# A convolution kernel's last stage: products of 64 rows in turn, and five groups finished by GpSimd

## What is computed

```python
residual = x                                    # result of the first layer, (4, 256, 64, 64)
h = relu(_bn_train(_conv(x, w1, 1, 0), g1, b1)) # 256 -> 64 channels
h = relu(_bn_train(_conv(h, w2, 1, 1), g2, b2)) # 3x3, 64 -> 64 channels
h = _bn_train(_conv(h, w3, 1, 0), g3, b3)       # 64 -> 256 channels, mean and variance over all positions
return relu(h + residual)
```

## Time and profile before

| | before |
|---|---|
| median of three runs | 842.15 us |
| profiled execution | 841.1 us |
| its span | 839.2 us |
| TensorE busy, share of the span | 94% |
| VectorE | 79% |
| ScalarE | 45% |
| GpSimd | 42% |
| mean granted clock of TensorE | 0.985 |

### The profile page before, as it was taken

One profiled execution on the slowest core, in us unless ns is written; L12 is line 12 of the kernel. 1 busy time (PEld: TensorE's weight loads), 2 busy tenths in 40 slices (PEclk: granted clock), 3 DMA queues, 4 the chain that ended last, 5 costly groups with the idle time before them and its releaser, 6 DMA issues.

```text
span 839.2 us, 13824 instructions
## 1 busy us (share of the span) xinstructions
PE 790.7 (94%) x4990; PEld 723.8 (86%) x4990; DVE 664.0 (79%) x916; ACT 378.6 (45%) x655; POOL 351.4 (42%) x255
## 2 busy tenths in 40 slices
PE   6799978999999999999999999999998879999896
PEld 2259978999999999999999999999987777777785
DVE  4988998897789589869968886896667466977796
ACT  2542112443353434434443443443345567727297
POOL 4245574384277248516823852484200013415300
PEclk9899999999999999999999999999999889999999
DMA  9922217967894997699589949648369989305398
GB/s 275 380 111 50 52 28 189 206 188 210 171 245 105 253 177 207 174 193 220 135 227 175 244 102 255 161 126 224 98 174 278 261 228 358 144 1 202 124 418 358
DMA packets 250108, 162.17 MB, mean 193 GB/s; under 512 B 191881, under 2 KB 232826, under 8 KB 247226
## 3 DMA queue, kind: packets, MB, share of 16 engines
q1 hardware_dynamic: 241050, 141.31, 64.2%
q10 hardware_dynamic: 8992, 19.99, 7.0%
HBM read 99.48 MB, written 56.36 MB: 186 GB/s over the span
## 4 chain that ended last, share of the span: by engine, by line
PE 79%; DVE 10%; issue 4%; DMA 3%; ACT 2%; SPq 1%; POOL 0%; DVEq 0%; ACTq 0%
PE ps L1265 22%; PE ps L1267 22%; PE ps L1266 22%; PE ps L1385 4%; PE ps L1401 3%; PE ps L1435 3%; DVE hT L2065 1%; DMA b2raw<-in_L_conv_b 1%; DMA xq<-in_x 1%; PE ps L1277 1%; DVE wpart L1723 1%; PE ps L1613 1%; DVE wsum L1723 1%; DVE xbuf L1793 1%; DMA yin<-y 1%
## 5 line engine op out<-in xcount | busy, mean ns | idle before, releaser
L849 POOL TENSOR_TENSOR ring<-whole,ring 128x576 fp32r<-128x576 f32 x112 | 195.2, 1748 | 288.8 <-ACT ring L932 288.8
L1265 PE MATMUL ps<-w_hi,ring 128*128 128x336 f32 x832 | 276.3, 332 | 10.7 <-POOL ring L849 4.4
L1267 PE MATMUL ps<-w_hi,ring 128*128 128x336 f32 x832 | 263.5, 317 | 0.0
L1266 PE MATMUL ps<-w_lo,ring 128*128 128x336 f32 x832 | 262.1, 315 | 0.0
L1265 PEld LDWEIGHTS ps<-w_hi,ring 128*128 128x128 f32 x832 | 157.9, 190 | 21.4 <-issue 14.0
L1266 PEld LDWEIGHTS ps<-w_lo,ring 128*128 128x128 f32 x832 | 157.7, 190 | 0.0
L1267 PEld LDWEIGHTS ps<-w_hi,ring 128*128 128x128 f32 x832 | 156.9, 189 | 0.0
L932 ACT ACTIVATE ring<-whole 128x576 fp32r<-128x576 f32 x112 | 87.1, 781 | 89.2 <-POOL whole L844 52.8
L932 ACT ACTIVATE band_hi<-ps 128x320 fp32r<-128x320 f32 (+1 forms) x128 | 53.1, 418 | 132.6 <-PE ps L1385 125.5
L1265 PE MATMUL ps<-band_hi,xT_hi 128*128 128x224 f32 (+2 forms) x320 | 95.2, 298 | 1.5 <-DVE xT_lo L1682 1.2
L1266 PE MATMUL ps<-band_lo,xT_hi 128*128 128x224 f32 (+2 forms) x320 | 92.9, 290 | 0.0
(11 more groups left out here) (217 smaller groups left out, 1372.3 us busy)
## 6 DMA issues: line engine op xcount, KB each, us to landing
xq<-in_x SPq DMA_DIRECT2D x116, 256.0 KB, 4.8
raw<-bands SPq DMA_DIRECT2D x32, 768.0 KB, 7.1
xbuf<-in_x SPq DMA_DIRECT2D x16, 1024.0 KB, 9.0
x_dram<-x ACTq DMA_DIRECT2D x32, 512.0 KB, 5.6
bands<-wide SPq DMA_DIRECT2D x64, 199.0 KB, 4.4
x1in<-x_dram SPq DMA_DIRECT2D x6, 2048.0 KB, 15.8
out<-x1in SPq DMA_DIRECT2D x12, 1024.0 KB, 4.3
bands<-wide SPq DMA_DIRECT2D x3, 1792.0 KB, 15.5
```

Source lines behind the costliest of these rows:

```text
L849: pool.tensor_tensor(split(k, 1), positions(whole[:, k % TBUFS, :], 0, 2), split(k, 0).bitcast(F32), ALU.subtract).then_inc(sig_lo_done, 1)
L1265: pe.matmul(dst, l_hi, r_hi_, start=first, stop=False, **kw)
L1266: pe.matmul(dst, l_hi, r_lo_, start=False, stop=False, **kw)
L1267: return pe.matmul(dst, l_lo, r_hi_, start=False, stop=last, **kw)
```

## The change

Three things are done together. The products are made over 64 rows: `last(p)` makes two groups 2p and 2p + 1 together, parity 0 on rows 0 to 63 and parity 1 on rows 64 to 127 of the array, a product of the one and a product of the other in turn, into different banks; the zeros take no part any more. The number of products stays 192. The call `last(1)` between the covariance product and the small products is gone: groups 0 and 1 both stand ahead of it. `f_done` counts pairs instead of groups.

Five groups (3, 9, 15, 21 and 27) are no longer added by VectorE. ScalarE evicts them from PSUM with scale and shift to one of two new tiles `evict` (signals `f_evicted`), GpSimd adds them to the residual and then takes the maximum with zero into the output place (signals `f_pool`). VectorE skips them. The order of groups on ScalarE stays.

All who waited for `f_added` or `f_out` now wait by `wait_added` and `wait_out`, which look at both counts: TensorE before it reuses banks, ScalarE and GpSimd before they write over the place of the unit before, SP before a store.

```diff
--- before.py
+++ after.py
@@ -225,6 +225,10 @@
         below = sb(l1y, "below", [P, 9, SPX])
         y1_2 = sb(l1y, "y1_2", [MID1, 2, HALF])
         l1y.close()
+        l1e = ExitStack()
+        below_hT = sb(l1e, "below_hT", [P, 8, SPX])
+        evict = sb(l1e, "evict", [P, 2, SPX])
+        l1e.close()
         y = sb(l1, "y", [P, 8, SPX])
         hT = sb(l1, "hT", [P, 2, 4, 2 * P], F32R)
         v3_hi = sb(l1, "v3_hi", [P, 2, C], F32R)
@@ -323,6 +327,7 @@
         relu2, h2_lo_done = sem("relu2"), sem("h2_lo_done")
         c2_done, c2_copied, c2_sum, c2_stat = sem("c2_done"), sem("c2_copied"), sem("c2_sum"), sem("c2_stat")
         vT_done, center_done, cov_zero, one_made = sem("vT_done"), sem("center_done"), sem("cov_zero"), sem("one_made")
+        f_evicted, f_summed, f_pool = sem("f_evicted"), sem("f_summed"), sem("f_pool")
         h2_hi_done = sem("h2_hi_done")
         hT_ps, hT_hi_done, hT_lo_done, gram_done = sem("hT_ps"), sem("hT_hi_done"), sem("hT_lo_done"), sem("gram_done")
         quad_ps, sums_ps = sem("quad_ps"), sem("sums_ps")
@@ -440,6 +445,35 @@
 
             at = (0, 4, 6, 2)[m % 4]
             return ps[:, at:at + 2, :]
+
+        BY_POOL_LAST = (3, 9, 15, 21, 27)
+
+        def by_pool(m):
+            return sum(j < m for j in BY_POOL_LAST)
+
+        def evicted(m):
+            return evict[:, by_pool(m) % 2, :].rearrange("p (b e) -> p b e", b=2)
+
+        def f_part(m):
+            u, h, a = m // 4, (m // 2) % 2, m % 2
+            return x1_place(u)[:, 2 * a:2 * a + 2, h * HALF:(h + 1) * HALF]
+
+        def f_place(m):
+            u, h, a = m // 4, (m // 2) % 2, m % 2
+            return out_place(u)[:, 32 * h + a:32 * h + 32:2, :].rearrange("p r (c b) -> p b r c", b=2)
+
+        def wait_added(eng, m):
+
+            if m in BY_POOL_LAST:
+                eng.wait_ge(f_evicted, by_pool(m) + 1)
+            else:
+                eng.wait_ge(f_added, m + 1 - by_pool(m))
+
+        def wait_out(eng, m):
+
+            eng.wait_ge(f_out, m + 1 - by_pool(m + 1))
+            if by_pool(m + 1):
+                eng.wait_ge(f_pool, by_pool(m + 1))
 
         def late(g, h):
 
@@ -557,7 +591,7 @@
         def store_out(sp, u):
             n, cb = u // 2, u % 2
             for h in range(2):
-                sp.wait_ge(f_out, 4 * u + 2 * h + 2)
+                wait_out(sp, 4 * u + 2 * h + 1)
                 sp.dma_start(out[n, cb * P:(cb + 1) * P, 32 * h:32 * h + 32, :],
                              out_place(u)[:, 32 * h:32 * h + 32, :]).then_inc(out_stored, 16)
 
@@ -925,6 +959,17 @@
                 pool.wait_ge(h2_hi_done, i + 1)
                 pool.tensor_tensor(h2_lo[:, i, :], y[:, i, :], h2_hi[:, i, :].bitcast(F32), ALU.subtract
                                    ).then_inc(h2_lo_done, 1)
+            for n, m in enumerate(BY_POOL_LAST):
+                pool.wait_ge(x1_back[m // 4], 48 if m // 4 == 7 else 16)
+                pool.wait_ge(f_evicted, n + 1)
+                pool.tensor_tensor(f_part(m), evicted(m), f_part(m), ALU.add).then_inc(f_summed, 1)
+                pool.wait_ge(f_summed, n + 1)
+                if m < 4:
+                    pool.wait_ge(hT_ps, 16)
+                    pool.wait_ge(h2_lo_done, 8)
+                else:
+                    wait_out(pool, m // 4 * 4 - 1)
+                pool.tensor_scalar(f_place(m), f_part(m).rearrange("p b (r c) -> p b r c", c=SW), 0.0, None, ALU.max).then_inc(f_pool, 1)
 
         @block.scalar
         def _(act):
@@ -1243,20 +1288,24 @@
             h2_high(7)
             root(3, BN3_ROOT)
             act.wait_ge(bn_dve, BN3_END)
-            for u in range(8):
+            for m in range(32):
+                u = m // 4
                 cb = u % 2
-                if u == 0:
+                if m in BY_POOL_LAST:
+                    act.wait_ge(f_done, m // 2 + 1)
+                    if by_pool(m) >= 2:
+                        act.wait_ge(f_summed, by_pool(m) - 1)
+                    act.activation(evicted(m), f_banks(m), ACT.Identity,
+                                   bias=shift[:, 2 + cb:3 + cb], scale=scale[:, 2 + cb:3 + cb]).then_inc(f_evicted, 1)
+                    continue
+                if m == 0:
                     act.wait_ge(hT_ps, 16)
-                else:
-                    act.wait_ge(f_out, 4 * u)
-                for k in range(4):
-                    h, a = divmod(k, 2)
-                    if u == 0 and a == 0:
-                        act.wait_ge(h2_lo_done, 6 + 2 * h)
-                    act.wait_ge(f_added, 4 * u + k + 1)
-                    act.activation(out_place(u)[:, 32 * h + a:32 * h + 32:2, :].rearrange("p r (c b) -> p b r c", b=2),
-                                   x1_place(u)[:, 2 * a:2 * a + 2, h * HALF:(h + 1) * HALF].rearrange("p b (r c) -> p b r c", c=SW),
-                                   ACT.Relu, bias=shift[:, 2 + cb:3 + cb]).then_inc(f_out, 1)
+                if m in (0, 2):
+                    act.wait_ge(h2_lo_done, 6 + m)
+                if m % 4 == 0 and m:
+                    wait_out(act, m - 1)
+                act.wait_ge(f_added, m + 1 - by_pool(m))
+                act.activation(f_place(m), f_part(m), ACT.Relu, bias=shift[:, 2 + cb:3 + cb]).then_inc(f_out, 1)
 
         @block.tensor
         def _(pe):
@@ -1648,18 +1697,22 @@
             gram(14)
             gram(15)
 
-            def last(m):
-                u, h, a = m // 4, (m // 2) % 2, m % 2
+            def last(p):
+                u, h = p // 2, p % 2
                 n, cb = u // 2, u % 2
-                if m == 3:
+                if p == 1:
                     pe.wait_ge(bn_dve, BN3_READ)
-                elif m >= 4:
-                    pe.wait_ge(f_added, m - 3)
+                elif p:
+                    for a in range(2):
+                        wait_added(pe, 2 * p - 4 + a)
+                cols, half = slice(cb * P, (cb + 1) * P), slice(h * HALF, (h + 1) * HALF)
                 for b in range(2):
                     sub = 2 * n + b
                     pe.wait_ge(h2_lo_done, sub + 1)
-                    mm = mm3(f_banks(m)[:, b, :], v3_hi[:, a, cb * P:(cb + 1) * P], v3_lo[:, a, cb * P:(cb + 1) * P],
-                             h2_hi[:, sub, h * HALF:(h + 1) * HALF], h2_lo[:, sub, h * HALF:(h + 1) * HALF], True, True)
+                    for i, (v, s) in enumerate(((v3_hi, h2_hi), (v3_hi, h2_lo), (v3_lo, h2_hi))):
+                        for a in range(2):
+                            rows = slice(64 * a, 64 * a + 64)
+                            mm = pe.matmul(f_banks(2 * p + a)[:, b, :], v[rows, a, cols], s[rows, sub, half], start=i == 0, stop=i == 2)
                 mm.then_inc(f_done, 1)
 
 
@@ -1667,14 +1720,13 @@
             pe.wait_ge(bn_dve, BN3_COV)
             pe.wait_ge(vT_done, 2)
             pe.matmul(ps[:, 3, 0:C], cov[:, :], vT[:, :], start=True, stop=True).then_inc(quad_ps, 1)
-            last(1)
             pe.wait_ge(bn_dve, BN3_QUAD)
             for cb in range(CB):
                 pe.matmul(ps[:, 3, C + 2 * cb:C + 2 * cb + 2], vT[:, cb * P:(cb + 1) * P], gm[:, 0:2], start=True, stop=True)
                 mm = pe.matmul(ps[:, 3, C + 4 + cb:C + 5 + cb], quad[:, cb * P:(cb + 1) * P], gm[:, 15:16], start=True, stop=True)
             mm.then_inc(sums_ps, 1)
-            for m in range(2, 32):
-                last(m)
+            for p in range(1, 16):
+                last(p)
 
         @block.vector
         def _(dve):
@@ -2174,13 +2226,14 @@
             link(dve.tensor_tensor(gm[:, 12:14], gm[:, 8:10], gm[:, 10:12], ALU.subtract))
             affine(2, 2, gm[:, 12:14], gm[:, 5:8:2], bn[:, 4:6], bn[:, 6:8], 3)
             for m in range(32):
-                u, h, a = m // 4, (m // 2) % 2, m % 2
+                u = m // 4
                 cb = u % 2
                 if m % 4 == 0:
                     dve.wait_ge(x1_back[u], 48 if u == 7 else 16)
-                dve.wait_ge(f_done, m + 1)
-                part = x1_place(u)[:, 2 * a:2 * a + 2, h * HALF:(h + 1) * HALF]
-                dve.scalar_tensor_tensor(out=part, in0=f_banks(m), scalar=scale[:, 2 + cb:3 + cb], in1=part,
+                if m in BY_POOL_LAST:
+                    continue
+                dve.wait_ge(f_done, m // 2 + 1)
+                dve.scalar_tensor_tensor(out=f_part(m), in0=f_banks(m), scalar=scale[:, 2 + cb:3 + cb], in1=f_part(m),
                                          op0=ALU.mult, op1=ALU.add).then_inc(f_added, 1)
```

## The result

| | before | after |
|---|---|---|
| median | 841.94 us (4 runs) | 860.89 us (4 runs, 859.94 to 861.69) |
| ratio to before | | 1.0221 (95% interval 1.0202 to 1.0241) |
| span of the profiled execution | 839.2 us | 859.0 us |
| TensorE busy | 94% | 91% |
| VectorE busy | 79% | 76% |

What follows compares the result with a forecast made beforehand. TensorE sets the last stage's pace, with other resources close. ScalarE then takes 38.4 + 5 x 4.4 - 4.8 = 55.6 us instead of 42.0, starting 0.35 us earlier: span 852.5 us, forecast 855.5 us, range 849 to 865 us.

Steps and rivals of the forecast that it cites:

- The wait of ScalarE: Last stage, before every fourth group: ScalarE waits for GpSimd's two passes, three gaps of about 4.4 us and two of 2.
- the maximum: GpSimd's second pass on each of five groups: 1.7 us; far from that, the forecast would be wrong.
- L: Time from the end of ScalarE's eviction to the end of GpSimd's maximum: 4.4 us, bounds 3.2 and 6.2 us.
- the add: GpSimd's first pass on each of five groups, adding the residual: 2.40 us.
- the upper bound of L: Both GpSimd passes at the add's time stretched by 23%, plus handovers: 6.2 us, giving 864.4 us.
- ScalarE's own work: ScalarE's 27 passes and 5 evictions in the last stage: 1.20 us a group, 38.4 us in all.
- The start: ScalarE's first pass of the last stage, after the covariance chain: 0.35 us earlier, at about 792.6 us.
- Rival 4: TensorE's clock falls in its new gaps: nothing much by itself, about 885 us only with serial halves; chance 0.01 at full price.
- The landing: From the end of ScalarE's last pass to the end of the span: stays 4.3 us.
- rival 2: Last stage's 64-row halves don't stream together: as the forecast but 1.4 us later at the start, 857 us; chance 0.08.
- rival 3: GpSimd is slowed by VectorE, L of 8.5 us: 876 us; chance 0.03.
- rival 1: Faster: GpSimd's tail is hidden and freed TensorE time comes through, up to the DMA stores' limit: 839.7 us; chance 0.03.

Runs made afterwards that it cites:

- first of four: Changed kernel, but the GpSimd groups are 4, 8, 16, 20, 28, with the wait for the unit before moved ahead of the eviction: 850.03 us in one run.
- early evictions: Changed kernel, but GpSimd groups are 4, 8, 16, 20, 28 and ScalarE evicts each two groups ahead of its turn: ratio to before 1.0039.
- pairs alone: Changed kernel with its 64-row products in pairs, but no group to GpSimd, VectorE adding all 32: ratio to before 0.9984, in a later set 1.0005.

## Why the prediction was right

**The wait of ScalarE: right.** Five gaps at the five places named, three long and two short by two passes, was the forecast; gaps of 5.53, 5.57, 5.81 and of 3.33, 3.29 us were found. Taking the wait off the path (first of four, early evictions) takes the loss off; taking GpSimd away takes all of it.

**Its size: the maximum was mis-sized.** Of L the add was right (2.40 us forecast, 2.39 us measured), the handovers were right (0.3 us), and the maximum took 2.83 us where I had 1.7 us from the select of 128 columns. A slope taken over 128 columns from a row of 0.29 us was too thin a base; the add of the same 1024 columns, which I had treated as an upper end of it, was nearer and still too low. L was 5.5 us instead of 4.4 us, and the gaps 23.5 us instead of 17.2 us. Of these 6.3 us, 5.7 us are the five longer L, 0.4 us the two passes that cover less than 2.4 us, and 0.3 us the longer last gap. The prediction named a maximum far from 1.7 us as a sign of being wrong, and it was met: the mechanism held, this term did not. The result lies in the range because the upper bound of L, 6.2 us, was wide enough. The prediction's estimate by the Trainium skill, "GPSIMD Engine Reference", sections 3.1 and 4.1 (one-input work roughly at line rate, 0.9 us), was further off: 2.77 us even on contiguous data.

**ScalarE's own work: 2.1 us too much.** It took 854.0 - 794.2 - 23.5 = 36.3 us, 1.13 us a pass. The 1.20 us that I had read off ten passes in a row was VectorE's pace showing through, not ScalarE's own. That pace is 1.19 us. The 1.23 us that I read off 16 groups is a mean of it and of the last three groups, which come 1.32 to 1.40 us apart, near TensorE's pace.

**The start: 1.6 us too early.** ScalarE's first pass came at 794.20 us instead of 792.6 us. The order was worth what was said only in part: with the clock held, as in pairs alone, the first pass is at c + 7.15 us against c + 7.30 us before, 0.15 us where I had 0.35 us. The covariance product did not keep its time as I had said: it starts at c + 1.41 us there, against c + 1.12 us before. In the changed kernel's profile the granted clock is 0.58 between 785.4 and 787.9 us, a mix of the two levels, and two products come 0.42 us apart from the next two instead of 0.23 us:

```profile
786.54 0.63 PE L1715 MATMUL ps<-h_hi,v_hi 64*128 64x512 f32 x2
786.96 0.63 PE L1715 MATMUL ps<-h_lo,v_hi 64*128 64x512 f32 x2
```

The first pass is then at c + 8.61 us. Rival 4 had the fallen clock at "nothing much"; here it costs some 1.5 us.

**The rest.** The landing took 859.0 - 854.0 = 5.0 us instead of 4.3 us. In sum 852.5 + 6.3 - 2.1 + 1.6 + 0.7 = 859.0 us, the span. That the last three terms come to 0.2 us is luck. The halves stream together, two products in 0.23 us, so rival 2 falls. In this the trace agrees with the Trainium skill, "TensorEngine Tiling (Array Packing)", Key Properties. GpSimd's add was not stretched by VectorE, 2.37 to 2.40 us in five rows (rival 3). The clock did fall in the gaps (rival 4), as the table after shows; beyond the start it cost nothing here, because the pairs made at the low clock were ready before GpSimd was. The bound that rival 1 was priced with, the stores, is what pairs alone ran into.

## What to carry to other kernels

Before a step is moved to an idle engine, write down who waits for it and what stands behind that wait in the waiting engine's queue: the latency of the detour counts there, once for each time, even if every engine is mostly idle. Five groups cost 19 us where they stood, 7 us as the first of their units and 3 us when fetched two groups ahead, by the times against before. And where resources lie close together, halving the work of the first buys at most the distance to the second. Here TensorE needs 32 x 1.40 = 44.8 us for the stage, the stores 40.2 us, VectorE 32 x 1.19 = 38.1 us and ScalarE 36.3 us; behind the halved TensorE the stores bind, and a pause of theirs is then not made up.

## What the runs showed of the hardware

- GpSimd's maximum against a constant over 128x1024 float32 took 2.83 us into an interleaved target and 2.77 us in place; its add of two tensors of that size took 2.39 us.
- Products of 64 rows on the two halves of the array, issued in turn into different banks, run at the same time: two in 0.23 us at a granted clock of 1.00 and in 0.42 us at 0.50.
- The granted clock fell at the start of the stage in some runs and not in others. In the changed kernel it is 0.58 from 785.4 to 787.9 us, with products over 128 rows 0.56 from 785.4 to 788 us; in pairs alone it is 1.00 there and 0.71 from 788 to 792 us. Between 782 and 785.4 us TensorE is busy for 1.4 us both before the change, where the clock then stayed at 1.00, and after it, where it fell. What decides it stays open.
- With the stores at a share of 1.01 of the DMA engines, 16.8 MB left at 417 GB/s, and the last store landed 7.1 us after its issue; the median of the stores was 4.5 us.
